# First attention: keys made already turned, values by products with 128 moving columns

## The reference, cut to what matters

```python
q = (text_hidden @ Wq).reshape(B, T_text, 16, 128)
k = (vision_tokens @ Wk).reshape(B, T_vis, 8, 128)    # each serves two query heads
v = (vision_tokens @ Wv).reshape(B, T_vis, 8, 128)
scores = einsum('bhtd,bhsd->bhts', q, k) / sqrt(128)
out = einsum('bhts,bhsd->bhtd', softmax(where(mask, scores, -inf)), v)
x = x + out.reshape(B, T_text, 2048) @ Wo
```

## Time and profile before

| | us |
|---|---|
| median of 3 runs | 2237.99 (2237.43 to 2243.26) |
| the profiled execution, in all | 2238.32 |
| its span | 2236.6 |
| PE busy | 2109.2 |
| DVE busy | 1562.8 |
| ACT busy | 1258.3 |
| POOL busy | 594.5 |

### The profile page before, as it was taken

The page is one execution under the profiler, slowest core; times in us unless marked ns, Lnnn a source line. Parts: engine busy times, 40 slices in busy tenths (PEclk is TensorE's granted clock), DMA queues, the critical chain, the costliest instruction groups (busy, mean ns, idle before and its releaser), DMA issues. The chain is left out here.

```text
span 2236.6 us, 37905 instructions
## 1 busy us (share of the span) xinstructions
PE 2109.2 (94%) x12062; PEld 1824.5 (82%) x12062; DVE 1562.8 (70%) x3783; ACT 1258.3 (56%) x3372; POOL 594.5 (27%) x1494
## 2 busy tenths in 40 slices
PE   5999999999999899998999999999999998599993
PEld 5899999999998678887788888888888887378882
DVE  6777777777778884444666677666766777867776
ACT  5554555445455533324666666666666666567772
POOL 1100010001001122223333434334343433145441
PEclk9999999999999999999999999999999999799997
DMA  6121112111210220002111111111112111278886
GB/s 242 65 93 69 66 52 80 47 70 50 76 66 20 71 76 1 1 1 76 48 57 48 59 65 57 47 57 47 57 47 69 63 39 39 85 264 290 291 282 257
DMA packets 75420, 194.98 MB, mean 87 GB/s; under 512 B 8432, under 2 KB 39176, under 8 KB 63008
## 3 DMA queue, kind: packets, MB, share of 16 engines
q1 hardware_dynamic: 65440, 172.55, 22.2%
q0 software_dynamic: 7680, 16.80, 2.2%
q10 hardware_dynamic: 2176, 4.19, 0.5%
HBM read 176.73 MB, written 25.17 MB: 90 GB/s over the span
## 5 line engine op out<-in xcount | busy, mean ns | idle before, releaser
L662 PE MATMUL bank<-l_wkv_hi,l_ctxT 128*128 128x256 f32 (+1 forms) x1024 | 277.9, 343 | 9.7 <-PEq L79 7.1
L1083 DVE TENSOR_TENSOR l_pT_lo<-bank,l_pT_hi 128x512 fp32r<-128x512 f32 x256 | 175.0, 683 | 70.9 <-ACT l_pT_hi L925 70.1
L1083 DVE TENSOR_TENSOR l_v_lo<-bank,l_v_hi 128x128 fp32r<-128x128 f32 (+1 forms) x256 | 91.6, 358 | 185.2 <-ACT l_v_hi L900 183.8
L662 PE MATMUL bank<-l_wo_hi,l_oT_hi 128*128 128x512 f32 x512 | 208.8, 408 | 0.7 <-DVE l_oT_lo L1083 0.7
L662 PEld LDWEIGHTS bank<-l_wkv_hi,l_ctxT 128*128 128x128 f32 x1024 | 181.7, 191 | 34.0 <-issue 8.2
L662 PE MATMUL bank<-xnT_hi,l_wq_hi 128*128 128x512 f32 x512 | 209.2, 409 | 0.0
L919 ACT ACTIVATE l_probs<-l_scored,l_nbias 128x256 f32<-128x256 f32 x256 | 128.2, 502 | 133.6 <-DVE l_nbias L1136 129.3
L662 PE MATMUL bank<-xnT_hi,l_wq_lo 128*128 128x512 f32 x512 | 200.8, 392 | 0.0
L662 PE MATMUL bank<-l_wo_hi,l_oT_lo 128*128 128x512 f32 x512 | 200.7, 392 | 0.0
L662 PE MATMUL bank<-xnT_lo,l_wq_hi 128*128 128x512 f32 x512 | 200.6, 392 | 0.0
L662 PE MATMUL bank<-l_wo_lo,l_oT_hi 128*128 128x512 f32 x512 | 200.5, 392 | 0.0
(11 more groups left out here) (287 smaller groups left out, 5911.2 us busy)
## 6 DMA issues: line engine op xcount, KB each, us to landing
l_ctxT<-ctx_split SPq DMA_DIRECT2D x63, 1024.0 KB, 4.8
moe_raw_gu<-in_L_ffn_gate_up_proj SPq DMA_DIRECT2D x32, 1024.0 KB
moe_raw_dn<-in_L_ffn_down_proj SPq DMA_DIRECT2D x32, 512.0 KB
l_raw_a<-in_L_xattn_Wq SPq DMA_DIRECT2D x16, 512.0 KB, 5.8
l_raw_a<-in_L_xattn_Wo SPq DMA_DIRECT2D x16, 512.0 KB, 5.4
x_sb<-in_x SPq DMA_DIRECT2D x4, 1024.0 KB, 8.7
moe_raw_gu<-moe_y_rows SPq DMA_DIRECT2D x4, 1024.0 KB
out_x<-x_sb ACTq DMA_DIRECT2D x8, 512.0 KB, 9.4
```

The source lines that it names most:

```text
L662: mm = nc.tensor.matmul(out, a[x], b[y], start=(i == 0), stop=(i == n - 1))
L1083: nc.vector.tensor_tensor(pair[1], src, pair[0].bitcast(F32), ALU.subtract).then_inc(done, 1)
```

## The change

In the first attention `project_kv`, `turn_k` and their copies are replaced. `project_v` makes the values of all four tiles one after another, context block stationary, 128 columns of `Wv` moving, into the four quarters of `b_kv[1]`: 24 products. `project_k` has the 128 columns of `Wk` stationary and 512 context columns moving, and makes the keys with features on partitions into `b_kv[0]`: 6 products, no transposes. `project_v` stands where `project_kv(0)`, `(1)` stood and `project_k` where `(2)`, `(3)` stood. ACT and DVE handle the values in one operation of 128x512 each (`copy_v`, `split_v`), `copy_k` waits for `project_k` and for `scores(3)`, and `kv_made` counts 2 for a body instead of 4. In the prologue `first_moments` comes behind `split_v`; before, it came behind the first `split_kv`. The second attention keeps its path.

```diff
@@ -434,6 +434,7 @@
         PROLOGUE = (0, -1)
+        KV = TG if rms else 2
...
@@ -500,7 +501,7 @@
                     if not over(hg, g + 2):
-                        sp.wait_ge(kv_made, count(TG, 2 * TG, hg, g))
+                        sp.wait_ge(kv_made, count(KV, 2 * KV, hg, g))
                         load_ctx(sp, g + 2)
@@ -695,6 +696,27 @@
+            def project_v(hg, g):
+                if over(hg, g + 1):
+                    return
+                pe.wait_ge(wkv_split, hg + (2 if g == NG - 1 else 1))
+                pe.wait_ge(ctx_in, count(16, 32, hg, g))
+                if g >= 0:
+                    pe.wait_ge(kv_split, count(1, 1, hg, g))
+                for t in range(TG):
+                    at = slice(P * t, P * (t + 1))
+                    mm = products(b_kv[1][:, at], [([ctxT[:, a, c, at] for a in range(2)], [w[:, c, kvw:2 * kvw] for w in wkv])
+                                                   for c in range(KC)])
+                mm.then_inc(kv_made, 1)
+
+            def project_k(hg, g):
+                if over(hg, g + 1):
+                    return
+                if g >= 0:
+                    pe.wait_ge(kT_split, count(1, 1, hg, g))
+                products(b_kv[0][:, :], [([w[:, c, 0:kvw] for w in wkv], [ctxT[:, a, c, :] for a in range(2)])
+                                         for c in range(KC)]).then_inc(kv_made, 1)
+
             def turn_k(hg, g):
@@ -780,15 +802,20 @@
-            for t in range(TG):
-                project_kv(*PROLOGUE, t)
+            if rms:
+                for t in range(TG):
+                    project_kv(*PROLOGUE, t)
+            else:
+                project_v(*PROLOGUE)
+                project_k(*PROLOGUE)
             project_q(*PROLOGUE, 0)
...
                 sum_q(0, 0, 0)
-            turn_k(*PROLOGUE)
+            if rms:
+                turn_k(*PROLOGUE)
             pe.sem_inc(pv_made, 2)
@@ -808,9 +835,11 @@
                             turn_late(0, 1)
-                    project_kv(hg, g, 0)
-                    project_kv(hg, g, 1)
-                    if not rms:
+                    if rms:
+                        project_kv(hg, g, 0)
+                        project_kv(hg, g, 1)
+                    else:
+                        project_v(hg, g)
                         turn_p(hg, g, 0)
@@ -820,9 +849,11 @@
                         weigh_v(hg, g, 0)
-                    project_kv(hg, g, 2)
-                    project_kv(hg, g, 3)
-                    if not rms:
+                    if rms:
+                        project_kv(hg, g, 2)
+                        project_kv(hg, g, 3)
+                    else:
+                        project_k(hg, g)
                         weigh_v(hg, g, 0)
@@ -838,8 +869,6 @@
                     scores(hg, g, 3)
-                    if not rms:
-                        turn_k(hg, g)
                     weigh_v(hg, g, 1)
@@ -899,10 +928,21 @@
+            def copy_v(hg, g):
+                if over(hg, g + 1):
+                    return
+                act.wait_ge(kv_made, count(KV, KV + 1, hg, g))
+                nc.scalar.copy(v[(g + 1) % 2][0][:, :, :].rearrange("p t d -> p (t d)"), b_kv[1][:, :]).then_inc(kv_hi, 1)
+
             def copy_k(hg, g, h):
...
                     return
-                act.wait_ge(k_turned, count(nkv, nkv + h + 1, hg, g))
+                if rms:
+                    act.wait_ge(k_turned, count(nkv, nkv + h + 1, hg, g))
+                else:
+                    act.wait_ge(kv_made, count(KV, KV + 2, hg, g))
+                    if g >= 0:
+                        act.wait_ge(s_made, count(UN, UN, hg, g))
                 if rms:
@@ -959,8 +999,11 @@
-            for t in range(TG):
-                copy_kv(*PROLOGUE, t)
+            if rms:
+                for t in range(TG):
+                    copy_kv(*PROLOGUE, t)
+            else:
+                copy_v(*PROLOGUE)
             for h in range(HB):
@@ -1006,19 +1049,22 @@
                             late(turned_high, 0, 1)
-                    copy_kv(hg, g, 0)
-                    copy_kv(hg, g, 1)
-                    if not rms:
+                    if rms:
+                        copy_kv(hg, g, 0)
+                        copy_kv(hg, g, 1)
+                    else:
+                        copy_v(hg, g)
                         if ending(hg, g):
...
-                    copy_kv(hg, g, 2)
-                    if not rms:
+                    if rms:
+                        copy_kv(hg, g, 2)
+                        copy_kv(hg, g, 3)
+                    else:
                         exponentials(hg, g, 2)
-                    copy_kv(hg, g, 3)
                     copy_p(hg, g, 1)
...
@@ -1093,6 +1139,12 @@
                 lo([w[:, t, :] for w in v[(g + 1) % 2]], b_kv[t % 2][:, kvw:2 * kvw], kv_split)
+
+            def split_v(hg, g):
+                if over(hg, g + 1):
+                    return
+                dve.wait_ge(kv_hi, count(1, 2, hg, g))
+                lo([w[:, :, :].rearrange("p t d -> p (t d)") for w in v[(g + 1) % 2]], b_kv[1][:, :], kv_split)
@@ -1216,9 +1268,11 @@
                         arrears(dve, i, probs[i % 2][:, :, :].rearrange("p t s -> p (t s)"))
-                split_kv(*PROLOGUE, t)
-                if AHEAD and t == 0:
-                    first_moments()
+                if rms:
+                    split_kv(*PROLOGUE, t)
+            if not rms:
+                split_v(*PROLOGUE)
+                first_moments()
             if rms:
@@ -1275,9 +1329,11 @@
                         split_p(hg, g, 0)
-                    split_kv(hg, g, 0)
-                    split_kv(hg, g, 1)
-                    if not rms:
+                    if rms:
+                        split_kv(hg, g, 0)
+                        split_kv(hg, g, 1)
+                    else:
+                        split_v(hg, g)
                         denominators(hg, g, 1)
...
```

More of the change, by code:

```diff
@@ L491, in _ @@
                 sp.wait_ge(k.ctx_stored, 16 * NG)
-            sp.wait_ge(kv_made, TG)
+            sp.wait_ge(kv_made, KV)
             load_ctx(sp, 1)
@@ L1058, in iteration @@
                     if g == 2 and not over(hg + 1, 0):
-                        weights_hi(wkv_flat, raw_b_flat, (wkv_in, hg * 32 + 64), (kv_made, count(TG, 2 * TG, hg, g)))
+                        weights_hi(wkv_flat, raw_b_flat, (wkv_in, hg * 32 + 64), (kv_made, count(KV, 2 * KV, hg, g)))
                     if not rms:
@@ L1289, in iteration @@
                         biases(hg, g, 2)
-                    split_kv(hg, g, 2)
+                    if rms:
+                        split_kv(hg, g, 2)
                     if not rms and g > 0:
@@ L1297, in iteration @@
                         rounds.raise_up(dve, rounds.magic[1], 0, 1)
-                    split_kv(hg, g, 3)
                     if rms:
+                        split_kv(hg, g, 3)
                         biases(hg, g, 2)
```

## The result

| | us | ratio to the kernel before, 95% interval |
|---|---|---|
| before (median of the 4 runs beside it) | 2239.76 (2237.43 to 2243.26) | |
| after | 2279.81 (2276.36 to 2281.91) | 1.0171 [1.0159, 1.0184] |
| predicted | 2269 (2256 to 2277) | |

What follows compares the result with a forecast made beforehand. The prediction took PE (TensorE), busy throughout the first attention's loop, as the bound. Price 22.2, waits 6.0, prologue 2.9 and first body -0.25 made +31 us on a median of 2238.0: 2269 us, range 2256 to 2277.

Steps and rivals of the forecast that it cites:

- TensorE's price: First attention's loop: 24 values' products at 0.112 us, six keys' at 0.229, `turn_k` gone: +0.74 us a body, 22.2 in all.
- The new wait: Before `weigh_v(2)`: without `turn_k` as cover PE waits for DVE's `split_p(2)`, 0.2 us a body (0 to 0.35), 6.0 in all.
- the head of DVE's chain: Behind `scores(3)`: DVE's chain to `split_p(2)` could begin only 0.08 to 0.1 us earlier, while PE comes 0.44 earlier.
- Ends of the stage: First attention's prologue +2.9 us, first body -0.25 us, last body unchanged.
- the remaining eleven products: Prologue's values' products from the 14th on: at 0.112 us from 32.41, the last starts at 33.5 us and ends at 33.8.
- the moments' way over POOL to ACT: Prologue: moments 3.1 us later, POOL and ACT follow, `copy_q(1)` at about 42.5 us, first scores about 45.9: +2.9 us.
- `project_v` hides in PE's idle time ahead of the first transposes: First body: `project_v`'s 1.23 us more lie in PE's idle 1.59 us there.
- Everything behind the stage shifted and otherwise as before: Behind the first attention: all code only starts later, with no change of its own, so nothing in the sum.
- The first: Rival: same PE price, no new wait, undisturbed prologue: 22.2 to 25 us more, 2260 to 2263 us; chance 0.20.
- The third: Rival: weight load mostly hidden, 0.081 us a product, body -0.01 us, prologue's share remains: 2241 to 2247 us; chance 0.05.
- fourth: Rival: weight load hidden, 128-column products cost their stream, 0.065 us, body -0.39 us: 2229 us, faster; chance 0.03.
- The second: Rival: 0.117 us a product and 0.35 us wait, or further half clock in the prologue: 2274 to 2280 us; chance 0.10.

Runs made afterwards that it cites:

- e7: The changed kernel with, in the prologue alone, `project_k` ahead of `project_v` and `first_moments` back ahead of `split_v`: 2276.38 us, ratio 1.016.
- e9: The changed kernel with values by wide products turned back, keys late, moments early, and 67 empty ScalarE increments behind the first attention: 2239.31 us, ratio 0.9994.

## Why the prediction was right and wrong

**TensorE's price: right.** 0.70 us a body, forecast 0.74: the values' products 2.63 us for 24 (forecast 2.69), the keys' 1.38 (1.37), `turn_k` 0.43 (0.44). The choice of 0.112 from the neighbours on both sides of 128 columns held: behind the first, the products start 0.112 us apart (303.15 to 305.61, 22 steps). The 64-column run shows the reason given, the load of the stationary block. The Trainium skill ("TensorE: Matmul & The Clock Gate", section "LDWEIGHTS (loading the stationary operand)") has P / 1.2 ns for a load of P columns, which makes an estimate of 107 ns for 128. By that rule, the trace agrees within 5 ns.

**The new wait: right in place and cause, a term that was sized too small.** Forecast 0.2 us a body, bounds 0 and 0.35; measured 0.305. It stands before `weigh_v(2)` for `l_pT_lo`, and cover for it takes it away whole. What was sized wrong is the head of DVE's chain. The forecast let it start 0.08 to 0.1 us earlier, since the addition ahead of it would end earlier. It did not: in both kernels the chain begins 0.47 us behind the last product of `scores(3)` (299.65 to 300.12 before, 315.51 to 315.98 after), now waiting for PE and not for the addition. 29 x 0.105 makes 3.0 us.

**Ends of the stage: a step that failed in the prologue.** The forecast priced the remaining eleven products there "With 0.112 us from 32.41 on", taking for granted that TensorE's clock comes back when it did before. In the changed kernel it came back 5.5 us later, and the products cost 0.21 each. The part of the step that I did work out, the moments' way over POOL to ACT, is real (3.0 us in the kernel before) but not additive: putting it back in the changed kernel left the first scores where they were. That the forecast of 2.9 us for the first scores came near the 4.1 measured is in part luck, since another delay than the one it names is enough for it. The head as a whole took 5.75 us instead of the 3.9 forecast, 1.85 more, which is about what two executions of the same prologue differ by. That `project_v` hides in PE's idle time ahead of the first transposes was right wherever no stretch at half clock lay there.

**"Everything behind the stage shifted and otherwise as before": the step that failed outright.** It stood in the sum as nothing. The second attention took 2.9 us more in the profiled execution, and padding alone makes that come and go. The forecast counted what ACT executes and not where its instructions lie. The changed kernel with the place put back measured 2273.24 us, inside the range that 2279.81 missed.

**Sum.** The span grew by 39.2 us: price 29 x 0.704 = 20.4 (forecast, cut in the same way, 21.5), wait 29 x 0.305 = 8.8 (5.8), head of the stage 5.75 (3.9), last two bodies 0 (-0.3), second attention 2.9 (0), the rest 1.4 (0). The last of these lies mostly between the second attention and the experts, and no run looked for its cause.

**Rivals.** The first expected no wait and an undisturbed prologue. The run with the keys' products moved shows the wait, and the first scores came 4.1 us late. The third and fourth fell with products 0.11 us apart. The second, given 0.10, came nearest in time. Its further stretch at half clock happened in this execution (48.1 to 51.5 us), but it named neither the longer first stretch nor the second attention, and its prices of 0.117 and 0.35 did not come.

**What stays open.** Why the clock comes back late. After PE's idle stretch in the prologue it came back 2.9 to 5.6 us after PE's first product in the seven kernels without 128-column products, and 8.0 to 11.5 us after it in the six that have them (one with 64 columns). Wide products placed first did not shorten it. The idle stretch was as long in all thirteen, 6.9 to 7.1 us, and no run varied it. Nor does the time of the fall sort them: the clock fell at 27.3 us both in e7, where it was back at 40.9, and in e9, where it was back at 34.1. This is a difference between kernels with one profiled execution each; no run shows what makes it. Within one form it varies too: with the same prologue the first scores came between 43.04 and 44.23 us. That ACT waits behind its branch for instructions to be fetched is inferred from the queue's packets, which rise and fall with it; no run shows a single fetch delaying a single instruction.

## What to carry to other kernels

Where products have few moving columns, count stationary blocks and not columns: in this kernel a product of 128 or 64 columns costs the 0.11 us of its block's load, one of 256 costs 0.12, and splitting one matrix of 256 moving columns into 128 plus a wide one adds loads even though the columns are the same. Work between a matmul and its successor is cover for the chain behind it; when you take it out, look at starts and not at busy time for what comes late. And when you change the number of instructions that an engine has ahead of a loop, look at the waits "issue" behind the branch and at the instruction queue's packets in the page: the same loop cost 2 to 21 us more at another place, and some empty instructions brought it back.

## What the hardware did that I had not expected

- ScalarE's loop of 217 instructions (its second attention) ran 31 bodies in 816 to 818 us behind 864 or 896 instructions, 819 to 822 us behind 781 or 909, 837.6 us behind 797; packets of the instruction queue 73 or 74 against 98 or 99. In the worst place each turn cost ACT 3.6 us with nothing to wait for, which lets PE wait and its clock fall to half for 3.4 us (four times).
- After equal idle stretches of about 7 us the granted clock came back 2.9 us behind PE's first product in one kernel and 8.0 to 11.5 us behind it in others, with PE busy all the time.
- A 128x128 block's load can hide beneath a product of 256 columns (0.12 us start to start) but not beneath one of 128 or 64: then the products start 0.112 us apart at 2.4 GHz and 0.21 at 1.2 GHz, however few the columns.
